# The last part of a two-layer network by one table of steps: eight attention steps moved among the expert groups, and a residual added by GpSimd

## The reference, cut to what matters

```
xn = layernorm(x)
# s: attention, 16 heads of 16 columns, on a second layernorm xn2 of xn
s = softmax(q @ k.T / 16) @ v + xn2
# f: top 2 of 8 experts per row, and a shared expert
f = sum_e w_e * ((xn @ W1[e]) * silu(xn @ W3[e])) @ W2[e]  +  shared(xn)
out = x + s * silu(f)          # silu(f) = f * (1 + tanh(f / 2)) / 2
```

## Time and profile before

| | us |
|---|---|
| median of 3 runs | 1671.74 (1670.36 to 1673.09) |
| the profiled execution | 1671.11 |
| its span, first to last instruction | 1669.4 |
| busy: TensorE / VectorE / ScalarE / GpSimd | 1505.7 / 1160.4 / 963.8 / 814.9 |

### The profile page before, as it was taken

One profiled execution on the slowest core, in us unless ns is written; L12 is line 12 of the kernel. 1 busy time (PEld: TensorE's weight loads), 2 busy tenths in 40 slices (PEclk: granted clock), 3 DMA queues, 4 the chain that ended last, 5 costly groups with the idle time before them and its releaser, 6 DMA issues.

```text
span 1669.4 us, 27215 instructions
## 1 busy us (share of the span) xinstructions
PE 1505.7 (90%) x9542; PEld 1128.7 (68%) x9542; DVE 1160.4 (70%) x1802; ACT 963.8 (58%) x1526; POOL 814.9 (49%) x755
## 2 busy tenths in 40 slices
PE   6589999999998379779999999999999999999976
PEld 3267877877787368647777777777777777777631
DVE  6667657757766388578776667777777777777657
ACT  3464565566454255434454567767677676777644
POOL 6424564554543278510255534656556655565410
PEclk9899999999999689969999999999999999999985
DMA  6716556553433579641455546766657677576563
GB/s 229 235 56 159 132 107 173 114 149 92 114 102 51 136 259 325 242 114 51 125 148 153 162 135 170 188 164 167 179 157 194 154 176 188 150 191 155 120 208 138
DMA packets 185384, 261.20 MB, mean 156 GB/s; under 512 B 36128, under 2 KB 117024, under 8 KB 185248
## 3 DMA queue, kind: packets, MB, share of 16 engines
q1 hardware_dynamic: 157216, 219.53, 43.8%
q0 software_dynamic: 28032, 39.93, 13.0%
HBM read 174.30 MB, written 84.56 MB: 155 GB/s over the span
## 4 chain that ended last, share of the span: by engine, by line
PE 39%; DVE 6%; SPq 3%; DMA 3%; issue 2%; ACT 2%; another core or an unknown queue 0%; POOL 0%; DVEq 0%; ACTq 0%; POOLq 0%
PE a_hidden_bank L93 16%; PE a_bank L93 8%; PE a_bank L1510 5%; PE a_max_bank L1479 5%; PE a_score_bank L1500 3%; DVE a_neg_max L1786 2%; DMA a_ka<-qk 2%; SPq L1259 1%; PE a_max_bank L1525 1%; SPq L1263 1%; PE a_bank L1517 1%; DVE a_w21lo L1827 1%; DVE a_hT1lo L1817 1%; ACT a_xThi L1665 1%; DVE a_w20lo L1827 1%
## 5 line engine op out<-in xcount | busy, mean ns | idle before, releaser
L1643 ACT ACTIVATE a_prob<-a_score_bank 128x1024 f32<-128x1024 f32 x240 | 246.2, 1026 | 244.7 <-PE a_score_bank L1500 198.6
L1786 DVE TENSOR_REDUCE a_neg_max<-a_max_bank 128x2 f32<-128x1024 f32 x249 | 304.1, 1221 | 82.4 <-PE a_max_bank L1479 70.5
L1416 POOL DMA_INDIRECT fs<-a_y,a_token x80 | 128.7, 1609 | 182.5 <-ACT a_y L1691 159.2
L619 POOL DMA_INDIRECT f<-e_ye,c_slot_row x64 | 104.6, 1635 | 128.7 <-ACT e_ye L530 65.6
L1479 PE MATMUL a_max_bank<-a_ka,a_qa 48*128 48x512 f32 x498 | 127.1, 507 | 27.8 <-DVE a_neg_max L1786 17.1
L1510 PE MATMUL a_bank<-a_prob,a_va 128*32 128x512 f32 x1024 | 143.3, 633 | 0.8 <-ACT a_prob L1643 0.6
L1809 DVE SCALAR_TENSOR_TENSOR a_tg<-a_tg,a_hidden_bank 128x512 f32<-128x512 f32 x112 | 76.7, 685 | 75.6 <-ACT a_tg L1653 71.0
L708 DVE TENSOR_TENSOR e_h<-e_bank,e_sge 128x512 f32<-128x512 f32 x64 | 44.3, 692 | 113.0 <-ACT e_sge L517 112.1
L1500 PE MATMUL a_score_bank<-a_qa,a_ka 50*128 50x512 f32 x480 | 100.5, 415 | 4.7 <-ACT a_prob L1643 2.4
L1479 PEld LDWEIGHTS a_max_bank<-a_ka,a_qa 48*128 48x128 f32 x498 | 47.5, 187 | 74.0 <-DVE a_neg_max L1786 31.1
L364 PE MATMUL e_bank<-m_wqkv,x_rows 128*128 128x512 f32 (+1 forms) x256 | 89.4, 492 | 4.6 <-ACT e_qkv L467 2.9
(11 more groups left out here) (370 smaller groups left out, 4909.1 us busy)
## 6 DMA issues: line engine op xcount, KB each, us to landing
a_raw<-in_W SPq DMA_DIRECT2D x120, 512.0 KB
e_raw<-in_w SPq DMA_DIRECT2D x48, 512.0 KB, 4.1
a_qa<-qk SPq DMA_DIRECT2D x192, 64.0 KB
a_ka<-qk SPq DMA_DIRECT2D x192, 64.0 KB
xs<-c_pad SPq DMA_DIRECT2D x20, 516.0 KB
a_xg<-xs SPq DMA_DIRECT2D x20, 516.0 KB
qk<-p_hi SPq DMA_DIRECT2D x32, 256.0 KB, 4.0
qk<-p_lo SPq DMA_DIRECT2D x32, 256.0 KB, 4.3
```

Of the source, the lines that this page charges most:

```text
L619: nc.gpsimd.indirect_dma_start(f_rows, bass.IndirectOffsetOnAxis(k.slot_row[:, e, t:t + 1], 0), ye[:, t, :], None, compute_op=ALU.add).the ...
L1416: nc.gpsimd.indirect_dma_start(f_rows, bass.IndirectOffsetOnAxis(token[x % 4][:, t:t + 1], 0), y[:, t, :], None, compute_op=ALU.add).then_ ...
L1643: nc.scalar.activation(prob[j % 2][:, 2 * p:2 * p + 2, :], score_bank(g, u)[:], ACT.Exp, scale=float(D) ** -0.5).then_inc(p_done, 1)
L1786: nc.vector.tensor_reduce(neg_max[:, g % 2, :, T * p + t], max_bank(g, m)[:], AX.X, ALU.max, negate=True).then_inc(mx_done, 1)
```

## The change

One table `steps` drives all five engines. It holds pairs (e, k) in order; after the expert groups 13, 15, ... 27 a pair (e, None) is put in, a step of attention without expert work. The place n in the table is attention's step, with g, u = divmod(n, 8). `made[n]` counts the maxima before step n. The table is cut at 256 steps, so that 24 steps stand after group 27 where 32 did. The waits are written anew with the same meaning. SyncE's pieces are tied to u or k each, so that their order shifts with the rests. At the end there are five buffers for the tanh, results are written in place into `k.rows`, GpSimd adds the residual of batches 0 to 6 after its loop, VectorE that of batch 7, all outputs wait for one semaphore, and the loads of `fs` are all issued at once.

```diff
-    AHEAD = 3
+    TH = len(th)
...
+    rests = range(NF - 15, NF, 2)
+    steps = []
+    for e in range(G):
+        steps += [(e, k_) for k_ in range(NU)] + [(e, None)] * (e in rests)
+    steps = steps[:NU * G]
+    made = [LEAD]
+    for e, k_ in steps:
+        made.append(min(made[-1] + {4: 2, 7: 0}.get(k_, 1), NU * G))
+    freed = steps.index((NF, 0))
...
 SyncE
-            for g in range(G):
-                e = g
-                if g + 2 < G:
-                    load_qk(g + 2)
-                store(e - 2, 1)
-                if group(e + 1):
-                    load_x(e + 1)
-                if NB <= e + 1 < NF:
-                    load_w(0, weights(e + 1, 0))
-                    load_w(1, weights(e + 1, 0))
...
+            for n, (e, k_) in enumerate(steps):
+                g, u = divmod(n, NU)
+                if u == 0 and g + 2 < G:
+                    load_qk(g + 2)
+                if u == 1 and g + 2 < G:
+                    load_v(g + 2)
+                if u == 3 and g + 1 < G:
+                    max_rows(g + 1)
+                if k_ == 0:
+                    store(e - 2, 1)
+                    if group(e + 1):
+                        load_x(e + 1)
+                    if e == NF + 1:
...
+                        for b in range(NB):
+                            sp.dma_start(tiles(x1[b]), at(x1_b, b)).then_inc(x1_in, 16)
+                if k_ == 2 and NB <= e + 1 < NF:
                     load_w(0, weights(e + 1, 0))
                     load_w(1, weights(e + 1, 0))
...
+                if k_ == 3 and NB <= e < NF:
                     load_w(2, weights(e, 0))
...
+                if k_ == 4:
+                    store(e - 1, 0)
+                if k_ == 4 and e == NF + 1:
                     sp.wait_ge(f_out, 16 * T * NX)
                     for b in range(NB):
-                        sp.wait_ge(fs_in[b % AHEAD], 16 * (b // AHEAD))
-                        sp.dma_start(tiles(fs[b]), at(fs_b, b)).then_inc(fs_in[b % AHEAD], 16)
+                        sp.dma_start(tiles(fs[b]), at(fs_b, b)).then_inc(fs_in[batch_set(b)], 16)
...
+                if k_ == 6 and NB <= e + 1 < NF:
                     load_w(0, weights(e + 1, 1))
                     load_w(1, weights(e + 1, 1))
-                if NB <= e < NF:
+                if k_ == 6 and NB <= e < NF:
                     load_w(2, weights(e, 1))
...
 GpSimd
+            for b in range(NB - 1):
+                if b == NB - 2:
+                    add_o(G - 1)
+                pool.wait_ge(fin_done, 2 * b + 2)
+                pool.wait_ge(x1_in, 16 * NB)
+                nc.gpsimd.tensor_tensor(k.rows[:, b], k.rows[:, b], tiles(x1[b]), ALU.add).then_inc(sum_done, 1)
...
 TensorE
+            for n, (e, k_) in enumerate(steps):
+                g, u = divmod(n, NU)
...
+                if k_ == 7 and group(e + 1):
                     transpose_x(e + 1)
+                if made[n + 1] > made[n]:
+                    maxima(made[n])
+                scores(g, u)
+                if u == 1 and g:
+                    weigh(g - 1, 3)
+                if u == 2 and g:
+                    transpose_o(g - 1)
+                if u == 3:
+                    transpose_max(g + 1)
+                if u in (4, 5):
+                    weigh(g, u - 4)
+                if u == 7:
+                    weigh(g, 2)
+                if k_ in (0, 2, 6) and group(e):
+                    up_gate(e, k_ // 2)
+                    up_value(e, k_ // 2)
...
+                if k_ in (1, 3, 5, 7) and group(e - 1):
+                    down(e - 1, k_ // 2)
...
 ScalarE
+            final = {freed + i: b for b, i in enumerate((15, 16, 17, 18, 20, 21, 22, 23))}
...
+                if n in final:
+                    half_tanh(final[n])
...
 VectorE
             def last(b):
                 dve.wait_ge(th_done, b + 1)
-                nc.vector.scalar_tensor_tensor(th[b % 2], th[b % 2], 1.0, fs[b], ALU.add, ALU.mult).then_inc(fin_done, 1)
+                nc.vector.scalar_tensor_tensor(th[b % TH], th[b % TH], 1.0, tiles(fs[b]), ALU.add, ALU.mult).then_inc(fin_done, 1)
                 dve.wait_ge(fin_done, 2 * b + 1)
                 dve.wait_ge(xa_done, NQ * (b + 1))
-                nc.vector.scalar_tensor_tensor(th[b % 2], th[b % 2], 0.5, flat(k.rows[:, b]), ALU.mult, ALU.mult).then_inc(fin_done, 1)
+                nc.vector.scalar_tensor_tensor(k.rows[:, b], th[b % TH], 0.5, k.rows[:, b], ALU.mult, ALU.mult).then_inc(fin_done, 1)
+                if b < NB - 1:
+                    return
+                dve.wait_ge(sum_done, b)
                 dve.wait_ge(fin_done, 2 * b + 2)
                 dve.wait_ge(x1_in, 16 * NB)
-                if b >= 3:
-                    dve.wait_ge(out_done[b % 3], 16 * (b // 3))
-                nc.vector.tensor_tensor(sums[b % 3], tiles(th[b % 2]), tiles(x1[b]), ALU.add).then_inc(sum_done, 1)
+                nc.vector.tensor_tensor(k.rows[:, b], k.rows[:, b], tiles(x1[b]), ALU.add).then_inc(sum_done, 1)
...
+            ending = {freed + i: b for b, i in enumerate((15, 17, 19, 21, 23))}
...
+                if u == 2 and g:
+                    divide(g - 1)
+                if u == 3:
+                    split_max(g + 1)
...
+                if n in ending:
+                    last(ending[n])
+            for b in range(5, NB):
+                if b == NB - 1:
+                    divide(G - 1)
+                last(b)
```

More of the change, by code:

```diff
@@ L1195, in layer1_attend_and_feed, with max_bank, score_bank @@
     LEAD = NU + 5
[L1197 to L1203, removed]
+    rests = range(NF - 15, NF, 2)
[7 more added lines that the diff above has]
+    freed = steps.index((NF, 0))
+    assert freed % 2 == 0
+    turned = [0] + [made[steps.index((e - 1, NU - 1))] for e in range(1, NF)]
+    def max_bank(i):
+        return GV if i < LEAD and i % 2 == 0 else M
+    def score_bank(n):
+        return GV if n >= freed and n % 2 else S2
     q_in, v_in, m_in, k_set = [sem(f"q_in{i}") for i in range(NR)], sem("v_in"), sem("m_in"), sem("k_set")
@@ L1470, in maxima @@
                     pe.wait_ge(q_in[q], 12 * 16 * (g // NR + 1))
[L1471 to L1476, removed]
+                if i >= LEAD:
+                    pe.wait_ge(mx_done, i)
+                elif i >= 2:
+                    pe.wait_ge(mx_done, i - 1)
+                if i:
+                    pe.wait_ge(x_lo, sum(turned[e] <= i for e in range(NF)))
                 for s in range(2):
                     rows = slice(HALF * s, HALF * s + K1)
-                    nc.tensor.matmul(max_bank(g, m)[:, s, :], qa[q][rows, p, t * P:(t + 1) * P], ka[q][rows, p, :], start=True, stop=True).then_inc(p1_ps, 1)
+                    nc.tensor.matmul(max_bank(i)[:, s, :], qa[q][rows, p, t * P:(t + 1) * P], ka[q][rows, p, :], start=True, stop=True).then_inc(p1_ps, 1)
             def transpose_max(g):
@@ L1567, in _ @@
             for m in range(NU):
-                maxima(0, m)
+                maxima(m)
             transpose_max(0)
[L1570 to L1622, removed]
+            for m in range(NU, LEAD):
+                maxima(m)
+            for n, (e, k_) in enumerate(steps):
+                g, u = divmod(n, NU)
+                if n == NU - 1:
                     pe.wait_ge(counted, 1)
@@ new lines, in _ @@
+            final = {freed + i: b for b, i in enumerate((15, 16, 17, 18, 20, 21, 22, 23))}
+            for n, (e, k_) in enumerate(steps):
+                g, u = divmod(n, NU)
+                fresh, coming = NB <= e < NF, NB <= e + 1 < NF
+                if k_ == 7 and group(e + 1):
+                    high_x(e + 1)
+                exps(g, u)
+                if u == 1 and g:
+                    copy_o(g - 1)
+                if k_ == 0:
+                    if group(e - 2):
+                        weighted(e - 2, 1)
+                    if group(e):
+                        tanh(e, 0)
+                    if fresh:
+                        high_w(0, weights(e, 1))
+                if k_ == 1:
+                    if group(e):
+                        high_h(e, 0)
+                    if fresh:
+                        high_w(1, weights(e, 1))
+                if k_ == 2:
+                    if e == 0:
+                        high_w(2, 0)
+                    if NB <= e - 1 < NF:
+                        high_w(2, weights(e - 1, 1))
+                    if group(e):
+                        tanh(e, 1)
+                if k_ == 3:
+                    if group(e):
+                        high_h(e, 1)
+                    if group(e - 1):
+                        weighted(e - 1, 0)
+                if k_ == 4:
+                    if group(e):
+                        tanh(e, 2)
+                    if coming:
+                        high_w(0, weights(e + 1, 0))
+                if k_ == 5:
+                    if group(e):
+                        high_h(e, 2)
+                    if coming:
+                        high_w(1, weights(e + 1, 0))
```

(48 more changed lines are left out.)

228 lines of the change are left out of this document (79 added, 149 removed).

## The result

The changed kernel takes 1729.56 us in the median of 4 runs (1728.22 to 1730.73) against 1671.05 for the kernel before on the same chip: ratio 1.0352, 95% interval 1.0333 to 1.037. It is slower by 58 us. The forecast was slower by 37, 1708 us, with a range up to 1722, so the direction was right and the size was not.

The account below looks back on a forecast made before the run. Stage one was taken as bound by TensorE's own instructions, the end by indirect adds, `fs` loads, tanh and VectorE. 1671.1 + 46.9 (stage one) - 9.8 (tail) = 1708.2 us, range 1678 to 1722.

Parts of the forecast that it names:

- Where the steps go, late loads: Stage one: loads of q and k come late in groups 14 to 16 and 20 to 23, 19.4 us in sum.
- the 0.9 of group 14: Stage one, after the first rest: keys at group 14 late by 0.9 us.
- The price of a rest: Stage one: eight rests at 2.85 us each, plus 1.8 us for two dearer ones, 24.6 us.
- The waits for the divide and for `split_max`: Stage one: waits behind `low_w2` also hit step k = 0 of groups 18 and 20, 1.5 and 1.4 us.
- Stage one: 24.6 + 2.9 + 19.4 = +46.9 us: Stretch with expert groups: rests 24.6, two waits at k = 0 2.9, late q and k loads 19.4 us.
- the short clock fall there: Tail, at the wait for `load_qk(31)`: the clock fall goes as that wait shrinks, 1 us gained.
- The tail: Group 28 to the end: `fs` comes sooner, GpSimd's adds and VectorE's products alternate; gives back 9.8 us.
- the six adds: Tail: GpSimd's six adds of 1024 columns and `add_o` alternate with ten VectorE instructions, 27.2 us, to 1648.4.
- The rival without blocking: Tail: GpSimd's and VectorE's chains run side by side, giving back 24.9 us: 1693 us; chance 0.14.
- Loads not late: Rival: in stage one only rests and the two waits count, +27.5, tail -9.8: 1689 us; chance 0.19.
- faster: Rival: rests cost 15 us with loads on time, the tail gives 24.9: 1661 us; chance 0.12.
- Dearer: Rival: both upper bounds hold, stage one +58, tail -2: 1727 us; chance 0.07.

Follow-up runs that it names:

- matmuls in 15 waits: Changed kernel with TensorE doing small matmuls of constants in six waits for late keys and nine further waits: 1727.20 us, ratio 1.034.
- rests in one block: Changed kernel with its eight rests in one block after expert group 13, 24 steps still in the last part: 1686.63 us, ratio 1.011.
- matmuls in 6 waits: Changed kernel with TensorE doing 12 to 30 small matmuls of constants in each of six waits for late keys: 1734.29 us, ratio 1.038.

## Why the prediction was wrong

- **Where the steps go, late loads.** Right in kind, and in six of seven places. Waits for `ka` came at k = 2 of group 15 (4.3 us, forecast 3.7), k = 1 of 16 (1.8; 4.2), k = 6 of 20 and 21 (3.4, 2.8; 2.6) and k = 5 of 22 and 23 (3.9, 3.1; 2.7). The sum over the kernel before is 16.8, forecast 19.4. The terms are further off than the sum, which is in part luck: the 0.9 of group 14 did not come and group 16 had 1.8 for 4.2, while groups 20 to 23 had 13.2 for 10.6, since the loads took up to 9.6 us from issue to maxima and not 8.7.
- **The price of a rest.** Right in kind, a little low. The first cost 2.61 us from maxima to maxima (1159.28 to 1161.89), forecast 2.85. The waits at all eight sum to 14.6 us, and with 11.8 us of matmuls (below) the rests cost 26.4, forecast 24.6. The waits for the divide and for `split_max` that hit a step k = 0 came at groups 19 and 21, not 18 and 20, and were 2.1 and 2.3 us, 4.4 in all, where I had 2.9.
- **The step that failed: "Stage one: 24.6 + 2.9 + 19.4 = +46.9 us".** The terms in it are waits and the rests' own matmuls. They measured 38.5 + 11.8 (605.6 - 593.8, from the kernel with matmuls in 15 waits) = 50.3. What was missing, a term put at nothing, is the speed of the work behind the waits: 624.3 - 605.6 = 18.7 us, which agrees with the 20 estimated from the time at half clock. I counted every matmul at the full clock, though the earlier trace rows showed one at 0.73 us instead of 0.50 just behind a wait of 3.61, and I had myself taken 1 us for "the short clock fall there" in the tail. More than ten such waits in a stage that had none had to be priced with it, and I priced them by their length alone.
- **The tail.** Gain 12.0, forecast 9.8. The tanh of batch 0 ends 38.8 us after the start of group 28 (1686.6 less 1647.8) where it ended after 45.8 before (1623.7 less 1577.9): 7.0 us sooner, forecast 8.6. From there to the end it took 40.7 us, forecast 44.5, so two errors of opposite sign meet in the 12.0; most of the second is in the stretch of the six adds, 23.9 us (1692.2 to 1716.1) for 27.2. GpSimd and VectorE alternated. The rival without blocking is out.
- **The rivals.** "Loads not late" fell by the waits; "faster" by stage one: even with rests in one block and little lateness they cost 28 us there, more than the tail gives. "Dearer", 1727, came nearest, for a reason that it did not name.
- **The range.** It had no clock term in its upper bound; with 18.7 more the sum is 1727.

## What to carry to other kernels

A stage that is bound by one engine has no room for moved work; what counts there is that work plus every wait that the shift of phase makes, so list for each load or hand-over what gates its issue in the queue and what needs it, before and after the shift. Where TensorE is the bound, price a new wait by its length and by slower matmuls behind it (the shortest with a fall behind it in stage one was 1.76 us in the change, and 1.66 us, before 1467.1, in the kernel without rests and with its adds on VectorE). Moving an elementwise step with two SBUF operands from VectorE to GpSimd saved nothing here while VectorE ran such steps too.

## What the runs showed of the hardware

TensorE's clock, after hundreds of microseconds at 2.4 GHz, fell to 1.2 GHz for 3.4 or 6.8 us during or right behind waits as short as 1.8 us (group 16: a wait of 1.76 before 1233.7, a fall at 1234.1). Not at each: those of 1.83 us before 1299.6 and of 2.33 before 1406.1 had no fall in the change, and the same two had one in the kernel with matmuls in 6 waits. Small products of constants in the waits kept it up: 44.4 us at half clock became 3.4 with 144 of them and none with 251. A product of 128 by 128 in float32 showed as two instructions of 0.112 us at 2.4 GHz. VectorE's product of 1024 columns with two SBUF operands took 3.27 us beside GpSimd's add and 1.22 alone, GpSimd's add 3.34 and 2.33.
